# Layer norms of a two-layer decoder: two small operations of the factors move from GpSimd to VectorE

## The reference

```
def _layernorm(x, axis=-1, eps=1e-05):
    m = jnp.mean(x, axis=axis, keepdims=True)
    v = jnp.var(x, axis=axis, keepdims=True)
    return (x - m) / jnp.sqrt(v + eps)

x = _layernorm(x + _L0_attn_ref(x, ...), axis=-1)           # norm 0
x = _layernorm(x + _L0_xattn_ref(x, ctx_1024, ...), axis=-1) # norm 1
x = _layernorm(x + _L0_ffn_ref(x, ...), axis=-1)            # norm 2
x = _layernorm(x + _L1_attn_ref(x, ...), axis=-1)           # norm 3
x = _layernorm(x + _L1_xattn_ref(ctx_1024, x, ...), axis=-1) # norm 4
x = _layernorm(x + _L1_ffn_ref(x, ...), axis=-1)            # norm 5
```

## Time and profile before

| | us |
|---|---|
| median of the runs | 1109.13 |
| the profiled execution | 1110.04 |
| its span, first to last instruction | 1108.3 |

### The profile page before, as it was taken

How to read it: one execution, slowest core, us unless ns; L and a number is a source line. 1 busy time by engine, 2 the same in 40 slices (tenths; PEclk the granted TensorE clock), 3 DMA queues, 4 the chain that set the end, 5 groups by cost and what they waited for, 6 DMA issues and landing times.

```text
span 1108.3 us, 17860 instructions
## 1 busy us (share of the span) xinstructions
PE 946.3 (85%) x5321; PEld 793.5 (72%) x5321; DVE 759.6 (69%) x1941; ACT 584.4 (53%) x1361; POOL 458.0 (41%) x536
## 2 busy tenths in 40 slices
PE   6999999999986899990776488877959999999994
PEld 5899999999964567770554478775737888888883
DVE  4666666666668553430468899935868989999894
ACT  3666666666655533440576444334635555555554
POOL 3566565656564213546884367743440000000002
PEclk8999999999997698995788678896979999999997
DMA  6223222223223101342210246301017666666551
GB/s 240 84 88 102 88 96 99 89 93 102 86 90 111 39 10 44 83 75 31 31 20 1 73 88 77 33 1 45 14 35 180 174 178 169 168 178 175 159 139 38
DMA packets 57457, 100.37 MB, mean 91 GB/s; under 512 B 7217, under 2 KB 34545, under 8 KB 57154
## 3 DMA queue, kind: packets, MB, share of 16 engines
q1 hardware_dynamic: 51362, 94.74, 30.8%
q0 software_dynamic: 6048, 5.05, 3.2%
HBM read 77.35 MB, written 22.41 MB: 90 GB/s over the span
## 4 chain that ended last, share of the span: by engine, by line
PE 39%; POOL 22%; issue 18%; DVE 13%; ACT 4%; DMA 3%; SPq 1%; POOLq 0%; ACTq 0%; DVEq 0%
PE PS L1658 8%; PE PS L1659 8%; PE PS L1660 8%; POOL P L624 7%; POOL Xp L706 4%; POOL WS L633 3%; PE PS L1854 3%; POOL WS L629 2%; DVE r0b L1473 2%; DVE rb L1486 2%; PE PS L1868 2%; POOL rs L420 1%; PE PS L1803 1%; PE PS L1809 1%; DMA Wb<-decay 1%
## 5 line engine op out<-in xcount | busy, mean ns | idle before, releaser
L624 POOL TENSOR_TENSOR P<-P,rl 128x256 f32<-128x256 f32 (+1 forms) x130 | 104.8, 827 | 121.6 <-DVE rl L1139 121.6
L417 POOL TENSOR_SCALAR ms<-mv 128x4 f32<-128x4 f32 x24 | 5.6, 232 | 307.2 <-DVE mv L410 298.5
L1057 ACT ACTIVATE FG<-PS 128x512 f32<-128x512 f32 x120 | 71.8, 598 | 111.3 <-PE PS L1660 111.3
L1132 DVE CUSTOM_DVE_ANT_0 P<-PS,cmask 128x128 f32<-128x128 f32 (+1 forms) x260 | 77.1, 352 | 70.6 <-issue 70.5
L850 ACT ACTIVATE P<-P,mn 128x128 f32<-128x128 f32 (+1 forms) x260 | 114.3, 444 | 1.9 <-DVE mn L1132 1.9
L1658 PE MATMUL PS<-XTh,W 128*128 128x512 f32 x256 | 101.7, 397 | 0.4
L1659 PE MATMUL PS<-XTl,W 128*128 128x512 f32 x256 | 101.1, 395 | 0.0
L1660 PE MATMUL PS<-XTh,W 128*128 128x512 f32 x256 | 101.0, 395 | 0.0
L1729 PE MATMUL PS<-VO,PT 128*128 128x128 f32 x804 | 100.6, 275 | 0.0
L1644 DVE TENSOR_TENSOR FU<-FG,PS 128x512 f32<-128x512 f32 x120 | 82.5, 688 | 25.4 <-PE PS L1660 25.4
L1729 PEld LDWEIGHTS PS<-VO,PT 128*128 128x128 f32 x804 | 95.0, 192 | 0.0
(11 more groups left out here) (426 smaller groups left out, 2683.4 us busy)
## 6 DMA issues: line engine op xcount, KB each, us to landing
GI<-coef SPq DMA_DIRECT2D x60, 256.0 KB, 4.1
GW<-coef SPq DMA_DIRECT2D x60, 256.0 KB, 4.2
w3s<-WS SPq DMA_DIRECT2D x32, 384.0 KB, 2.6
W<-w3s SPq DMA_DIRECT2D x32, 384.0 KB, 3.2
Wb<-decay SPq DMA_DIRECT2D x7, 1024.0 KB, 14.9
WR<-in_w SPq DMA_DIRECT2D x32, 192.0 KB, 2.5
WR<-in_w SPq DMA_DIRECT2D x16, 256.0 KB, 2.8
w12f<-WS SPq DMA_DIRECT2D x16, 256.0 KB, 2.1
```

Source lines behind the costliest of these rows:

```text
L624: last = pool.tensor_tensor(v, v, f, ALU.mult)
L1057: act.activation(FG[:, k % 2, :], bank(4 + k % 2), ACT.Silu).then_inc(sem("fg_done"), 1)
L1132: dve.tensor_tensor_reduce(out=P[:, slot, c:c + w], in0=scores(par, q), in1=cmask[:, 256 - w:256], scale=1.0, scalar=3e38, op0=ALU.add, op ...
```

## The change

`ms` and `nm` are computed by VectorE, directly behind the last `bn_aggr` of a chunk, in a new function `ln_shift`. The last `bn_aggr` raises a new semaphore `ln_ag`, for which VectorE itself waits before the two operations; the second of them raises `ln_mv`. GpSimd keeps the power (L420) and the product (L422), and one of its two waits for its own semaphore. Norm 3's own statistics get the same call. `turn(n, c)` is only the number of the chunk, 4n + c.

```
@@ -401,6 +401,9 @@
+        def turn(n, c):
+            return NC_ * n + c
+
         def ln_stats(dve, n, c, src=None):
@@ -408,21 +411,25 @@
             for t in tiles(c):
                 dve.wait_ge(sem("ln_st"), T * n + t + 1)
                 last = dve.bn_aggr(mv[:, t, :], st[:, t, :])
-            last.then_inc(sem("ln_mv"), 1)
+            last.then_inc(sem("ln_ag"), 1)
+            ln_shift(dve, turn(n, c), slice(4 * c, 4 * c + 4))
+
+        def ln_shift(dve, k, cc):
+
+            dve.wait_ge(sem("ln_ag"), k + 1)
+            dve.tensor_scalar(ms[:, cc], mv[:, cc, 1], LN_EPS, None, ALU.add)
+            dve.tensor_scalar(nm[:, cc], mv[:, cc, 0], -1.0, None, ALU.mult).then_inc(sem("ln_mv"), 1)
 
         def ln_factors(pool, n, c):
 
-            cc, k = slice(4 * c, 4 * c + 4), NC_ * n + c
+            cc, k = slice(4 * c, 4 * c + 4), turn(n, c)
             pool.wait_ge(sem("ln_mv"), k + 1)
-            pool.tensor_scalar(ms[:, cc], mv[:, cc, 1], LN_EPS, None, ALU.add).then_inc(sem("ln_factor"), 1)
-            pool.tensor_scalar(nm[:, cc], mv[:, cc, 0], -1.0, None, ALU.mult).then_inc(sem("ln_factor"), 1)
-            pool.wait_ge(sem("ln_factor"), 4 * k + 2)
             pool.tensor_tensor(rs[:, cc], ms[:, cc], neghalf[:, cc], ALU.pow).then_inc(sem("ln_factor"), 1)
-            pool.wait_ge(sem("ln_factor"), 4 * k + 3)
+            pool.wait_ge(sem("ln_factor"), 2 * k + 1)
             pool.tensor_tensor(nb[:, cc], nm[:, cc], rs[:, cc], ALU.mult).then_inc(sem("ln_factor"), 1)
 
         def ln_norm(act, n, c, src=None):
-            act.wait_ge(sem("ln_factor"), 4 * (NC_ * n + c) + 4)
+            act.wait_ge(sem("ln_factor"), 2 * turn(n, c) + 2)
@@ -1494,7 +1501,8 @@
                 if b % 2:
-                    last.then_inc(sem("ln_mv"), 1)
+                    last.then_inc(sem("ln_ag"), 1)
+                    ln_shift(dve, turn(3, b // 2), slice(2 * b - 2, 2 * b + 2))
```

## The result

| | before | after |
|---|---|---|
| median of six runs each, us | 1109.55 (1107.23 to 1112.29) | 1101.16 (1098.72 to 1105.11) |
| ratio, with its 95% interval | | 0.9928 [0.9903, 0.9954] |
| the profiled execution | 1110.04 | 1104.72 |
| its span | 1108.3 | 1103.0 |

The change makes the kernel 8.4 us faster. I had forecast 1103.9 with a range from 1101.8: the direction was right, the size too small, and the median lies 0.6 under the range. That miss is smaller than the uncertainty of the measurement, since the interval of the ratio corresponds to 1098.8 to 1104.4. The profiled execution is among the longer ones of the changed kernel, and its own difference, 5.3, says less than the median.

A forecast was written before the change was run, and what follows sets the result against it. The bound differs by norm: GpSimd (1, 5, 4 with VectorE close), ScalarE (0), gather landing (2), VectorE (3). Gains 0.7 + 1.6 + 0.7 + 0.35 + 0.2 + 1.6 = 5.2 us give a median of 1103.9, range 1101.8 to 1107.4.

The forecast's parts named there:

- The collision: VectorE's new `ms` and `nm` wait for GpSimd's running power or product; total gain 5.2 us instead of 6.4.
- the rival's: Where powers run, GpSimd's power does not hold VectorE; sum 6.4 us, time 1102.7; chance 0.22.
- Norm 5: Last norm, paced by GpSimd: ScalarE's step falls from 2.02 to 1.60, gain 1.6 us; 2.2 if nothing is held.
- Norm 1: GpSimd alone sets the pace: steps of 3.89 fall by 0.62, gain 2.2 us, less 3 x 0.2 for waits: 1.6.
- Norm 2: Landing of gathers hides the first two chunks' factors, 0.06 gained each; only the third's pay fully: 0.7 us.
- Norm 0: ScalarE sets the pace after its second chunk: 0.33 from the first chunk plus 0.37 idle time, gain 0.7 us.
- Norm 3: State scans: VectorE pays 2 x 0.30; chunk 1's factors return 0.62, chunk 3's 0.33; net gain 0.35 us.
- The part that was to pay: In norm 3, chunk 1's factors, for which ScalarE waits while GpSimd is not idle, gain 0.62 us.
- Norm 4: Bound passes from GpSimd (2.02 a step) to VectorE (2.05): first chunk gains 0.33, three steps lose 0.03 each; gain 0.2 us.
- a microsecond or two either way: Rival: something outside the norms moves, above all stretches with TensorE at its lower clock; chance 0.08.
- 13.5 x 0.1 or 1 us more: Allowance for the range's lower end, 1101.8: no waits on GpSimd, and VectorE paying 0.2 a chunk instead of 0.30.
- x: Time VectorE pays per chunk for the two added operations: forecast 0.30 us, lower end 0.2, upper end 1.1.

The follow-up runs named there:

- the third trace: The changed kernel measured once more, with nothing altered, for a third trace; median 1100.65 us, ratio 0.9925 to the kernel before.

## Why the prediction fell short

**The step that failed is "The collision"**: "A VectorE tensor_scalar from tile to tile in SBUF evidently waits for a GpSimd operation that is under way." L1611 (L1619 after the change) is held again, 0.996, 0.982 and 0.974 in the three traces of the changed kernel, but by a tensor_tensor of 128x512. I carried that over to the power because both are GpSimd's tensor_tensor by name. The power lasts 1.01 on 4 elements per partition and holds nothing. By it I took 0.6 each from norms 1 and 5. Without it my sum was 6.4, the rival's, and the time 1102.7; at equal clock the whole measured 6.6 +- 0.3. That agreement is closer than the terms, so it is in part luck:

- Norm 5: forecast 1.6, without the collision 2.2; 2.2 in the traces (9.62 and 9.64 to 7.40) and 2.3 at equal clock. The step fell to ScalarE's 1.42, as the 1.40 without collision.
- Norm 1: forecast 1.6, without 2.2; the trace of norm 1 alone has 2.5. I counted 0.62 a chunk from the start of `ms` to that of the power. Between GpSimd's power L694 and the next L420 lay 0.70 (358.06 to 358.76), and now nothing lies there (356.33 + 1.04 = 357.37, next start 357.35). So the 0.08 ahead of `ms` went as well, which I had not counted; why the power starts without such a gap is not shown, since `ms` had one though its input was ready too. With 0.03 less for the power the step fell by 0.77. At equal clock 1.5 +- 0.3 of the 2.5 is left, and I can't say where the rest went.
- Norm 2: the mechanism was right. The wait for the landing sets the gathers' pace:

```profile
521.01 1.54 POOL L713 DMA_INDIRECT Xp<-yrows,pidx  x1 [0.30 <-issue]
521.99 1.63 POOL L427 TENSOR_TENSOR rs<-ms,neghalf 128x4 f32<-128x4 f32 x1
523.71 0.20 POOL L429 TENSOR_TENSOR nb<-nm,rs 128x4 f32<-128x4 f32 x1
524.58 1.62 POOL L713 DMA_INDIRECT Xp<-yrows,pidx  x1 [0.67 <-DMA Xp<-yrows,pidx]
```

  The last gather ends at 522.55 and the next starts 2.03 later, released by the DMA after 0.67 of idle time, where before it was GpSimd's own issue, 2.18 after the gather's end (525.61 to 527.79). That gives 0.15 a wait instead of 0.06. In all it is 105.1 from the first gather to `AB` with norm 2 alone, before 106.2 and 106.1: 1.0 to 1.1 for the forecast's 0.7.
- Norm 0: forecast 0.7; the stretch has 0.84 less, as told, and the medians show nothing.
- Norm 3: forecast 0.35, 0.9 in the trace with norms 3 and 4. The 0.30 a batch was 0.29 in eight of twelve batches and 0.68 in four, and behind the loop the factors gave 1.5 where I had 0.62 + 0.33. Batch 4 of the changed kernel, one of the four:

```profile
671.86 0.17 DVE L420 TENSOR_SCALAR ms<-mv 128x4 f32<-128x4 f32 x1
671.94 0.17 DVE L421 TENSOR_SCALAR nm<-mv 128x4 f32<-128x4 f32 x1
672.01 1.22 DVE L1485 SCALAR_TENSOR_TENSOR dfb<-PS,r0b 128x1024 f32<-128x1024 f32 x1
...
673.37 0.71 PE L1951 MATMUL PS<-WUr,dsel 128*128 128x256 f32 x4 [0.67 <-DVE dfb L1485]
...
675.48 1.23 PE L1963 MATMUL PS<-WUr,dsel 128*128 128x256 f32 x4 [1.39 <-DVE rb L1493]
...
676.84 2.29 DVE L1493 TENSOR_TENSOR_SCAN rb<-PS,gb 128x1024 f32<-128x1024 f32 x1 [0.30 <-PE PS L1963]
```

  L1963 takes 1.23 here, with a granted clock of 0.55 from 675 to 677. In batch 6 of the third trace it takes 0.74 after the same idle time (1.40), with 0.97, and that batch lasts 14.12. So VectorE, which had no idle time here, waits 0.30 for a TensorE at its lower clock. The part that was to pay did: chunk 1's factors start at once behind GpSimd's sum (713.04).
- Norm 4: forecast 0.2, nothing to be seen in the trace. Its steps are 2.05 as forecast, VectorE the bound:

```profile
763.33 1.01 POOL L427 TENSOR_TENSOR rs<-ms,neghalf 128x4 f32<-128x4 f32 x1 [6.94 <-DVE nm L421]
...
765.38 1.01 POOL L427 TENSOR_TENSOR rs<-ms,neghalf 128x4 f32<-128x4 f32 x1 [0.76 <-DVE nm L421]
```

**The second thing that was missing is the clock**, and the sum had no term for it. I gave it a chance of 0.08 and "a microsecond or two either way". The whole change ran at a mean clock of 0.9085 against 0.9047, worth 2.1 us, and that is what carries the median below the range: dropping only the collision would have given 1102.7, inside it. The whole change had the higher clock beside the kernel before in both measurements that list both (0.9078 against 0.9047, 0.9103 against 0.9065). Norms 0, 1 and 5 together have 0.9092, but 0.9065 is the value beside them too; each of the three alone has no higher clock. Why it rises is open. The stretch from `SE` to `FL` gains 1.6 to 2.0 in four of nine traces and 0.2 at most in the other five, so it is part of the answer at most.

The lower end of the range was also drawn too high: "13.5 x 0.1 or 1 us more" is 1.35, which from 1102.7 gives 1101.4. The measured 1101.16 lies under that too, and x was 0.28, not the 0.2 of that end.

The Trainium skill's rule ("SBUF — State Buffer", "Who interferes with whom") that I drew on is borne out by the sums of norm 3 (1.41 to 1.69) and by L1611. It did not show against the power, for any of the three forms, and there the measurement decides (0.145 to 0.170 inside the power).

## What to carry to other kernels

A stall seen once belongs to the pair of operations that made it: before carrying it over to another pair, place a probe of a few lines inside the other operation. Where an engine executes small operations one behind the other, what moving some of them away frees is the distance from the end of the work before to the first operation that stays, gaps included. When a stretch of two traces is compared, start it behind TensorE's work where that can be done: norm 5 seemed to gain 2.8 and gained 2.2. And where a kernel's single runs follow the granted clock, compare variants at equal clock: here the parts then added up to the whole within their errors, while the medians of the whole had 1 to 2 us more.

## What was unexpected in the hardware

- GpSimd's power of 128x4 (1.01) does not hold a VectorE tensor_scalar of 128x4 or 128x64 (0.15 to 0.17 inside it); a GpSimd sum of 128x1020 holds even one of 128x4 with every second element as its source until it ends (1.68).
- The power's row starts while a gather is still being issued on the same engine (521.99, the gather from 521.01 to 522.55) and lasts 1.63. It ends 1.07 after the gather, about its usual 1.01, so nothing is won by the early start.
- Where the tiles lie in SBUF is worth about as much as the whole change (6.4 +- 0.5 against 6.6 +- 0.3 at equal clock): 704 bytes in front of most tiles shorten the products of the last loop, 87 or 88 in 20 us without them, 90 with them, and with the products the kernel by 6 to 7 us. Which tiles' addresses matter I did not find out.
- One kernel does not have one speed: the mean granted clock of single runs of the kernel before went from 0.897 to 0.915, with times from 1114.56 to 1104.72.
